# Four double transfers instead of eight, one raising instruction, and a later MLP addition in a fused hyperbolic attention and MLP loop

## What is computed

```
# hyperbolic attention: 16 heads of 8 features, N = 256
diff_sq  = |q|^2 + |k|^2 - 2 q.k
denom    = max((1 - |q|^2) * (1 - |k|^2), 1e-6)
dist     = arccosh(max(1 + 2 * diff_sq / denom, 1))
attn     = softmax(-dist)
x        = x + (attn @ v) @ wo.T
# MLP
x        = x + relu(layernorm(x) @ w1 + b1) @ w2 + b2      # width 512
```

## Time and profile before

| | |
|---|---|
| runs without profiler | 2449.48, 2448.92, 2444.56 us; median 2448.92 |
| the profiled execution | 2456.33 us, its span 2454.2 us |
| mean granted TensorE clock | 0.907 of full speed |
| the fused loop | from about 1370 us to the end, 32 batches |
| one batch in the middle of it | 32.4 to 34.3 us |
| transfers `u<-spare` | 256 of 512 KB, 36864 packets, median 12.2 us from issue to landing |

### The profile page before, as it was taken

One profiled execution on the slowest core, in us unless ns is written; L12 is line 12 of the kernel. 1 busy time (PEld: TensorE's weight loads), 2 busy tenths in 40 slices (PEclk: granted clock), 3 DMA queues, 4 the chain that ended last, 5 costly groups with the idle time before them and its releaser, 6 DMA issues. The chain is left out here.

```text
span 2454.2 us, 50808 instructions
## 1 busy us (share of the span) xinstructions
PE 2089.9 (85%) x15438; PEld 1566.8 (64%) x15438; DVE 1956.8 (80%) x5939; ACT 1767.4 (72%) x3085; POOL 1627.2 (66%) x1866
## 2 busy tenths in 40 slices
PE   4999999999999996999997677777777778777876
PEld 4677777777777775888885445555555555555554
DVE  4677776776777774778775899999999999999992
ACT  2666666666666762444432799999999999999996
POOL 2776676766666750000001899999999999999993
PEclk7999999999999996999997579888888988889888
DMA  5000000000000003353450466776666777666674
GB/s 142 1 2 2 2 1 2 2 1 2 1 2 1 2 2 70 86 119 76 96 114 10 93 127 130 139 138 128 124 119 127 141 141 134 119 129 124 129 142 80
DMA packets 81388, 184.24 MB, mean 75 GB/s; under 512 B 9479, under 2 KB 31530, under 8 KB 81195
## 3 DMA queue, kind: packets, MB, share of 16 engines
q0 software_dynamic: 36864, 134.23, 29.1%
q1 hardware_dynamic: 36010, 43.38, 7.9%
q10 hardware_dynamic: 8320, 4.19, 0.7%
HBM read 42.85 MB, written 4.72 MB: 19 GB/s over the span
## 5 line engine op out<-in xcount | busy, mean ns | idle before, releaser
L1557 POOL TENSOR_TENSOR spare<-spare,u 128x1024 f32<-128x1024 f32 x192 | 456.2, 2376 | 16.0
L542 ACT ACTIVATE prob<-s_ps,nmax 128x128 f32<-128x128 f32 (+1 forms) x1024 | 364.4, 432 | 132.2 <-DVE nmax L599 132.2
L599 DVE CUSTOM_DVE_ANT_0 s_ps<-s_ps,mask 128x128 f32<-128x128 f32 (+1 forms) x1024 | 340.7, 385 | 100.7 <-issue 76.4
L1633 DVE TENSOR_SCALAR u<-d_ps 128x1024 f32<-128x1024 f32 x256 | 312.1, 1219 | 48.7 <-PE i_ps L1374 48.1
L579 POOL TENSOR_TENSOR g_lo<-g_all,g_hi 128x512 fp32r<-128x512 f32 x256 | 329.1, 1286 | 21.4
L1637 DVE SCALAR_TENSOR_TENSOR u<-i_ps,u 128x1024 f32<-128x1024 f32 x256 | 313.5, 1225 | 13.2 <-DVE u L1633 0.5
L1374 PE MATMUL d_ps<-rowsT 28*128 28x256 f32 x1024 | 144.7, 357 | 149.5 <-DVE u L1637 145.9
L534 ACT COPY g_all<-g_ps 128x512 f32<-128x512 f32 x256 | 151.5, 592 | 162.6 <-PE g_ps L63 161.5
L1514 ACT ACTIVATE u<-u 128x1024 f32<-128x1024 f32 x256 | 257.0, 1056 | 1.7 <-DMA u<-spare 1.6
L1517 ACT ACTIVATE u<-u 128x1024 f32<-128x1024 f32 x256 | 255.7, 1051 | 0.0
L1374 PEld LDWEIGHTS d_ps<-rowsT 28*128 28x128 f32 x1024 | 92.4, 208 | 246.3 <-issue 241.7
(11 more groups left out here) (275 smaller groups left out, 5795.2 us busy)
## 6 DMA issues: line engine op xcount, KB each, us to landing
u<-spare POOLq DMA_DIRECT2D x256, 512.0 KB, 12.2
w_all<-w_rows SPq DMA_DIRECT2D x128, 256.0 KB, 5.9
x<-L_attn_x ACTq DMA_DIRECT2D x8, 512.0 KB, 13.9
y<-x SPq DMA_DIRECT2D x32, 128.0 KB, 10.0
wkqv<-L_attn_Wkqv SPq DMA_DIRECT2D x4, 528.0 KB, 8.9
gate_rows<-L_ffn_gate_proj SPq DMA_DIRECT2D x1, 512.0 KB, 14.4
up_rows<-L_ffn_up_proj SPq DMA_DIRECT2D x1, 512.0 KB, 11.1
down_cols<-L_ffn_down_proj SPq DMA_DIRECT2D x1, 512.0 KB, 13.0
```

The source lines that it names most:

```text
L542: last = nc.scalar.activation(prob[:, kind, at, :].rearrange("p c n -> p (c n)"), s_ps[kind][:, at.start * P:at.stop * P], ACT.Exp, bias=n ...
L599: last = nc.vector.tensor_tensor_reduce(out=scores, in0=scores, in1=keep.mask[:, N - width:N], scale=-1.0, scalar=3.4e38, op0=ALU.add, op1 ...
L1557: nc.gpsimd.tensor_tensor(extra, extra, pair, ALU.mult).then_inc(prod_done, 1)
L1633: nc.vector.tensor_scalar(u[:, slot(i, p), :], d_ps[:, :], 0.0, None, ALU.max).then_inc(dist_done, 1)
```

## The change

Three edits, all in the fused loop.

1. **Sums by two.** `pool_sum` now moves two neighbouring pairs in one transfer of 1 MB (8 KB in each partition), waits for the root of the second of them, and signals one semaphore for both; there are four semaphores instead of eight, and whoever waits for a pair waits for the transfer with both. SUMS_BEHIND issues pairs (0,1), (2,3), (4,5) behind product 5. The fourth, (6,7), is issued in the next batch's body, behind its product 0; for the last batch it stands behind the loop. `pool_norm4` follows sum (4,5) directly.
2. **Raising in one.** L1554 and L1555 become a single tensor_scalar over 1024 columns; the tile `twos` goes.
3. **Addition later.** VectorE's `dve_y` moves from step 1 to step 2, behind the copy of row block 7.

```
-    SUMS_BEHIND = {5: (0, 1, 2, 3, 4, 5, 6, 7)}
+    SUMS_BEHIND = {5: (0, 2, 4)}
-        sum_landed = [S_(f"sum_landed{n}") for n in range(HP)]
+        sum_landed = [S_(f"sum_landed{n}") for n in range(HP // 2)]
-            after(engine, sum_landed[p], 16 * (b + 1))
+            after(engine, sum_landed[p // 2], 16 * (b + 1))
...
         def pool_sum(pool, b, p, i):
-            pool.wait_ge(root_done, b * HP + p + 1)
-            nc.gpsimd.dma_start(u[:, slot(i, p), :], spare[:, p, :], accum_op=ALU.add).then_inc(sum_landed[p], 16)
+            pool.wait_ge(root_done, b * HP + p + 2)
+            at = slot(i, p)
+            nc.gpsimd.dma_start(u[:, at:at + 2, :], spare[:, p:p + 2, :], accum_op=ALU.add).then_inc(sum_landed[p // 2], 16)
...
-            nc.gpsimd.tensor_tensor(extra[:, 0:4], pair[:, 0:4], twos[:, :], ALU.add)
-            nc.gpsimd.tensor_scalar(extra[:, 4:2 * W2], pair[:, 4:2 * W2], 1.0, 2.0, ALU.mult, ALU.add).then_inc(raised, 1)
+            nc.gpsimd.tensor_scalar(extra, pair, 1.0, 2.0, ALU.mult, ALU.add).then_inc(raised, 1)
...
                     for p in PRODUCTS:
                         pool_product(pool, b, p, i)
+                        if p == 0 and one_before:
+                            pool_sum(pool, b - 1, HP - 2, (i - 1) % TURN)
                         if p == NORM_BEHIND and two_after:
                             pool_norm(pool, b + 2)
                         for n in SUMS_BEHIND.get(p, ()):
                             pool_sum(pool, b, n, i)
-                            if n == NORM4_BEHIND and three_before:
-                                pool_norm4(pool, b - 3, i)
+                        if p == NORM4_BEHIND and three_before:
+                            pool_norm4(pool, b - 3, i)
                 written_out(body)
+                pool_sum(pool, END, HP - 2, END % TURN)
...
-                        if p == 1 and five_before:
+                        if p == 2 and five_before:
                             dve_y(dve, b - 5)
```

More of the change, by code:

```diff
@@ L1272, in hyperbolic_attention_and_mlp @@
         attnT = m.sb("attnT3", [P, N])
-        twos = m.sb("twos", [P, 4])
         part_stats = m.sb("part_stats3", [P, TURN, TB, 6])
@@ L1879, in _ @@
                 nc.gpsimd.memset(v[:, :, :, :, DH:VW], 1.0).then_inc(zeroed, 2)
-                nc.gpsimd.memset(twos[:, :], 2.0).then_inc(v_cleared, 1)
                 nc.gpsimd.memset(eps[:, :], LN_EPS).then_inc(rows_set, 1)
                 nc.gpsimd.memset(xh4[:, :, :, :], 1.0).then_inc(rows_set, 1)
-                pool.wait_ge(v_cleared, 3)
                 pool.wait_ge(rows_set, 2)
@@ L1892, in body @@
                             pool_sum(pool, b, n, i)
-                            if n == NORM4_BEHIND and three_before:
-                                pool_norm4(pool, b - 3, i)
+                        if p == NORM4_BEHIND and three_before:
+                            pool_norm4(pool, b - 3, i)
                 written_out(body)
+                pool_sum(pool, END, HP - 2, END % TURN)
                 for b in (END - 2, END - 1, END):
                     pool_norm4(pool, b, b % TURN)
-                for p in range(HP):
+                for p in range(0, HP, 2):
                     wait_sum(pool, END, p)
```

## The result

The changed kernel takes 2476.5 us, the median of 6 runs (2466.9 to 2480.1), against 2449.2 us for the kernel before (6 runs, 2444.6 to 2456.2): a ratio of 1.010, 95% interval 1.0077 to 1.0122. It is slower, by about 25 us (25.3 between the means, 27.3 between the medians). I had forecast 2452 and given 0.33 to slower; the time lies above my range. The profiled execution took 2480.1 us, with a span of 2478.2, 24.0 us longer than before.

A forecast was written before the change was run, and what follows sets the result against it. A ring of ScalarE, TensorE and VectorE was taken to set the period, GpSimd being full but late for nobody. 0 + 0 + 1.2 + 2.2 = +3.4 us on 2448.9 gave 2452 us, range 2442 to 2467.

The forecast's parts named there:

- Part 1, the raising: On GpSimd, one instruction fewer per product saves about 1.0 us per batch, ending in idle time; 0 on the time.
- Part 2, descriptors: On GpSimd, a two-pair transfer takes one descriptor time of 0.9 us, saving 3.6 us per batch; 0 on the time.
- Rival (a): Two-pair transfers need 1.8 us of descriptors, so landings come 0.7 us later and logarithms wait: 2462 us, chance 0.14.
- Part 2, the rate: On the DMA engines, 8 KB pieces move at the rate of 4 KB ones, 2.73 us per pair.
- Rival (b): DMA rate 10% lower with 8 KB pieces, so Ln(6) waits: about +30 us, time 2482, chance 0.06.
- a margin of nothing for Ln(6): Mid-loop, ScalarE's Ln(6) must also await sum 7: margin falls from 2.6 us to nothing; 0 on the time.
- The first three batches: At the loop's start, Ln(6) waits for sum 7: 2.4 us if ScalarE sets the end, 0 if VectorE; +1.2 taken.
- Part 3, the direct price: On VectorE, the later addition costs 0 in a fast batch and +0.24 us in a slow-clock one.
- Part 3, the step that failed: On VectorE, the +0.24 us falls on 9 of the 27 batches with this addition: +2.2 us.
- (c): Fewer batches with TensorE at 1.2 GHz: six fewer of 11 gives 2442.5 us; chance 0.12, of it 0.10 faster.
- the slower half: The other direction of (c): six more batches with TensorE at 1.2 GHz, slower by as much; no chance given to slower.
- (d): GpSimd sets the period after all: a twentieth of its 4.6 us per batch passed on, 7 us, time 2445; chance 0.08.

The follow-up runs named there:

- E3: The kernel before with only the raising done in one instruction: 2446.8 us, ratio 1.0000.
- E2: The changed kernel with the addition put back to VectorE's step 1: 2447.8 us, ratio 1.0000.
- E4: The kernel before with only the sums by two: 2446.9 us, ratio 1.0006.
- E9: The changed kernel with one keep-busy matmul added in TensorE's step 6: 2436.9 us, ratio 0.9968.
- E7: The kernel before with one keep-busy matmul added in TensorE's step 6: 2432.3 us, ratio 0.9947.
- E12: The changed kernel with the addition back in step 1 and one keep-busy matmul in TensorE's step 6: 2431.8 us, ratio 0.9949.
- E14: The kernel before with two small unused memsets added in VectorE's step 2: 2472.3 us, ratio 1.0106.
- E1: The kernel before with only the addition moved to VectorE's step 2: 2466.3 us, ratio 1.0079.
- E5: The changed kernel with the addition ahead of the copy of row block 7 in VectorE's step 2: 2472.8 us, ratio 1.0105.
- E13: The changed kernel with VectorE's copy of row block 7 moved from step 2 to step 3: 2443.1 us, ratio 0.9975.
- E17: The kernel before with TensorE's values of group 0 waiting for VectorE's first tile copy of the next batch: 2452.6 us, ratio 1.0039.
- E10: The kernel before with two small unused copies with a factor added in VectorE's step 2: 2533.3 us, ratio 1.0364.
- E8: The kernel before with two keep-busy matmuls added in TensorE's step 6: 2433.1 us, ratio 0.9942.
- E16: The kernel before with one keep-busy matmul in step 6, two in step 4, and row block 7's copy in step 3: 2428.3 us, ratio 0.9926.

## Why the prediction was wrong

**Part 1, the raising: right.** E3 is 1.0000, and GpSimd's gain in the changed kernel went into idle time, nearly all put down to VectorE, as said.

**Part 2, descriptors: right.** I took one descriptor time for a transfer of two pairs. GpSimd's rows of the changed kernel, by shape, and the first and the last issue of a batch as single landings (issues: KB, us to landing):

```profile
L1547 POOL DMA_DIRECT2D u<-spare x128 | 112.6, 893 | 55.0 <-ACT spare L1500 49.5 <-issue 4.8 <-ACT u L1505 0.7
```

```profile
u<-spare POOLq DMA_DIRECT2D x1, 1024.0 KB, 7.1
...
u<-spare POOLq DMA_DIRECT2D x1, 1024.0 KB, 11.6
```

893 ns for an issue, half as many packets (36864 before, 18432 now) for the same 134.23 MB. A transfer of 1 MB is 144 packets, 9 on each of 16 engines. That agrees with the Trainium skill, DMA: Bandwidth & Descriptors, section The descriptor swizzle, by which each engine gets eight data descriptors and one for completion; 128 of the 144 are then 8 KB each. The packet of preferably at most 4096 bytes, in the section SWDGE vs HWDGE vs iDMA of that page of the Trainium skill, led to no cutting here. Rival (a) falls.

**Part 2, the rate: right.** The queue's packets took 29.1% of 16 engines' 2454.2 us before, 11427 us or 0.31 us for each of 36864, and take 26.9% of 2478.2 us now, 10666 us or 0.58 us for each of 18432: 7% less in all. Rival (b) falls. The Trainium skill, DMA: Bandwidth & Descriptors, section SDMA does more than copy, gives 2048 elements as the most; a row of two pairs has just that many, and its packets show no price for it. In the batch from 1904.91 the sums are issued from 1908.19 to 1918.91 and the last lands at 1918.91 + 11.6 = 1930.5, 22.3 us behind the first issue. I had feared a margin of nothing for Ln(6) in a fast batch. It starts at 1932.28, 1.8 us after the landing: the eight pairs are down 22.3 us behind the first issue, where they took 23.9 before.

**The first three batches: too dear.** I had set +1.2 us. All waits of L1513 for transfers are 0.7 us in the whole program, less than the 1.6 of before. E2 and E4 show no price.

**Part 3, the direct price: borne out as far as it can be told.** I set +0.24 us for a slow batch and 0 for a fast one. The like slow batch went from 34.00 to 34.29 us. The fast one went from 32.37 to 32.57 in the changed kernel, but in E9 and E7, where the stretch behind the std row is at full clock, fast batches take mostly 32.4 to 32.6 in both. Over nine batches that is about the +2.2 us that stood in the sum. The 5 us between E9 and E12 hold more than that, the batches of 33.8 us among them, so they don't contradict it and don't confirm it.

**Part 3, the step that failed.** The working said "Such waits occur 4 times in 12 batches, so 9 times in the 27 batches that have this addition: +2.2 us". This holds the share of slow-clock batches fixed while VectorE's step 2 is made longer. It isn't fixed: a lateness of 0.1 to 0.3 us in step 2 (E14, E1) is enough to move the low stretches, and one matmul in TensorE's idle time (E7, E9) to take them away. Behind the std row the loop went from one low stretch of some 6.8 us and a short one of 3.4 in three batches to two of 6.8, with a third kind of batch, 3.4 us more per three batches. Over 27 batches that is 27 / 3 x 3.43 = 31 us against a loop that keeps to 32.37, 34.00 and 32.61 throughout; the real loop before has some batches of 34.0 more, and 24.7 us were measured from the first std row to the last. I had the mechanism among the rivals, as (c), with "Six more would be slower by as much. Nothing in the rows says which", and then gave its 0.12 to the faster side alone. That was the error that the text itself could have shown: a rival of two directions with an unknown sign needs a chance on both. By its own price, 1.6 us for each batch more, even the slower half (about 2462) would have been too small, since the new slow batches cost up to 3.2 us over a fast one (35.55 against 32.37): besides the stretch at steps 7 and 0 there is the low clock at the batch's very start. The kernel before has that from 1600 to 2350 us in two batches alone, those of 33.9 us that start at 1797.49 and 2295.82.

**(d)** is refuted by E2, which has the 4.6 us less of GpSimd per batch: it asked for 7 us, 0.3%, and the ratio is 1.0000 (0.9988 to 1.0012).

**Open.** Why just this shift leads to this order of batches is not shown; E5 leads to another one as costly, E13, with a shift the other way, to a good one, and E17, by its times and clocks, to either, from run to run. Whether E1 is faster than the whole change (1.0079 against 1.010) isn't told by the intervals: E1's loop leaves the costly order for some batches and the changed kernel's doesn't. Moving TensorE's wait for the addition from the values of group 0 to those of group 1 wasn't tried: VectorE would then read the bank `o_ps` while TensorE writes it.

## What to carry to other kernels

Where TensorE's granted clock goes up and down inside a loop that hands TensorE work in pieces, read it first, by place within the batch and over several batches, before adding up tenths of a microsecond: here 0.1 to 0.3 us of work in VectorE's step 2 cost 19 to 27 us (E1, E14, the change), mostly by moving the low stretches, and one matmul put into idle time took 13 to 16 us from the kernel before and 40 from the changed one. A cost worked out in the old pattern holds only if the pattern does, so try the edit also with the clock's low stretch filled; that tells its own price. Size a probe from its own rows before you read its result: E10's two small instructions held VectorE up by 1.8 us where 0.26 were meant. And an engine that is 96% busy but late for nobody gives nothing back when it is relieved: look for who waits for it.

## What the runs showed of the hardware

- The low stretches lock to the loop: in the changed kernel the same three batch lengths (32.57, 35.55, 34.29) repeat from body 7 to 29, and in the rounds from 1904.91 and from 2007.32 us the stretches stand at the same distance from the std row within 0.1 us. TensorE is busy 78 to 80% of the time there, in pieces, with waits of up to 1.9 us for VectorE and 2.3 for ScalarE between them. The Trainium skill, TensorE: Matmul & The Clock Gate, section A second HAM failure mode: psum-queue depth-cycling, tells of a kernel whose short idle times between groups of matmuls keep the clock going up and down. The trace agrees in that (0.50 and 1.00 in turn), and E14 adds that such a loop can have a cheap and a costly rhythm for nearly the same work.
- Which idle time is filled matters: one matmul at step 6 (E7) gives 0.9947 and two there (E8) 0.9942, the same, while two more at step 4 (E16) raise the mean granted clock from 0.930 to 0.944 and give no time.
- A small `tensor_scalar` from SBUF to SBUF on VectorE lasted until GpSimd's instruction beside it ended: in E10 each of 128x64 values took 0.18 to 2.37 us, and the pair held up VectorE by 0.3 to 2.4 us. A memset of the same size took 0.11 us each of 54 times (E14), with GpSimd as busy.
- A transfer that adds 1 MB to SBUF from GpSimd's queue takes one descriptor time of 0.89 us with 8 KB in a partition, as one of 512 KB does with 4, and its packets took 7% less time for the same bytes (10666 against 11427 us).
